# A spectral convolution on one core: the delayed odd spectrum by a table of phases on VectorE in place of a third second-step product

## The reference, cut to what matters

```python
def _stu_conv(phi, u, n):            # n = 8192
    sgn = +1 on even positions, -1 on odd ones
    Vf = rfft(phi, n); Uf_p = rfft(u, n); Uf_m = rfft(u * sgn, n)
    U_plus = irfft(Vf * Uf_p)[:sl];  U_minus = irfft(Vf * Uf_m)[:sl] * sgn
out = sum_k s_k (U_plus_k @ Mpp_k + U_minus_k @ Mpm_k) + sum_i shift(u, i) @ Mu_i
```

## Time and profile before

| what | us |
|---|---|
| median of 3 runs | 3136.38 |
| lowest and highest of them | 3129.91, 3153.72 |
| the profiled execution, its own time | 3149.02 |
| the span of its trace | 3147.3 |

### The profile page before, as it was taken

How to read it: one execution, slowest core, us unless ns; L and a number is a source line. 1 busy time by engine, 2 the same in 40 slices (tenths; PEclk the granted TensorE clock), 3 DMA queues, 4 the chain that set the end, 5 groups by cost and what they waited for, 6 DMA issues and landing times. The chain is left out here.

```text
span 3147.3 us, 88222 instructions
## 1 busy us (share of the span) xinstructions
PE 2528.9 (80%) x36744; PEld 1963.3 (62%) x36744; DVE 1538.8 (49%) x3563; ACT 1355.0 (43%) x2712; POOL 258.7 (8%) x477
## 2 busy tenths in 40 slices
PE   0565999545429999999999999999796884999999
PEld 0334888522128888888888888888633751555555
DVE  6441344233506565656565656565411343466666
ACT  0562344155016565656565656566410354232332
POOL 0102112000010000000000000000012001101000
PEclk9866899677859999999999999999998776799999
DMA  6437556422451111111111111110178520000000
GB/s 201 124 97 121 106 106 115 117 119 102 128 138 45 41 41 41 41 41 41 41 41 42 41 41 41 41 41 21 51 265 285 176 61 12 9 22 19 22 17 27
DMA packets 189043, 242.48 MB, mean 77 GB/s; under 512 B 36891, under 2 KB 147278, under 8 KB 185146
## 3 DMA queue, kind: packets, MB, share of 16 engines
q1 hardware_dynamic: 154325, 124.05, 14.7%
q0 software_dynamic: 30368, 94.52, 11.1%
q10 hardware_dynamic: 3969, 18.31, 1.5%
HBM read 145.54 MB, written 91.27 MB: 75 GB/s over the span
## 5 line engine op out<-in xcount | busy, mean ns | idle before, releaser
L962 DVE COPY spc_g<-spc_pz 128x512 f32<-128x512 f32 x1088 | 670.8, 683 | 446.8 <-PE spc_pz L860 446.7
L940 ACT ACTIVATE spc_g<-spc_pz 128x512 f32<-128x512 f32 x1088 | 587.2, 612 | 345.6 <-PE spc_pz L860 343.7
L860 PE MATMUL spc_pz<-spc_v,spc_as 108*128 108x128 bf16 x8704 | 599.9, 222 | 38.6 <-issue 27.7
L860 PEld LDWEIGHTS spc_pz<-spc_v,spc_as 108*128 108x128 bf16 x8704 | 515.2, 99 | 132.8 <-issue 46.0
L878 PE MATMUL spc_pz<-spc_g,spc_u 128*20 128x128 f32 x17408 | 503.7, 274 | 31.7 <-DVE spc_g L962 18.2
L878 PEld LDWEIGHTS spc_pz<-spc_g,spc_u 128*20 128x20 f32 x17408 | 480.0, 134 | 64.6 <-ACT spc_g L940 41.3
L1602 DVE SCALAR_TENSOR_TENSOR moe_yt<-moe_ex,moe_gb,moe_yt 128x128 f32<-128x128 f32 x768 | 209.6, 344 | 146.7 <-ACT moe_yt L1506 145.7
L845 PE MATMUL spc_pu<-spc_f,spc_s 128*128 128x256 f32 x816 | 222.6, 399 | 71.8 <-DMA spc_s<-s_sf 71.8
L1456 PE MATMUL moe_ex<-moe_ew,moe_d 128*128 128x512 f32 x512 | 254.0, 619 | 16.8 <-DVE moe_yt L1602 16.8
L507 DVE SCALAR_TENSOR_TENSOR inv_xo<-inv_pa,inv_mask,inv_xo 128x256 f32<-128x256 f32 x256 | 123.6, 484 | 222.7 <-PE inv_pa L465 163.9
L485 ACT ACTIVATE inv_b<-inv_pb 112x1024 f32<-112x1024 f32 x128 | 125.2, 1021 | 221.1 <-PE inv_pb L444 221.1
(11 more groups left out here) (195 smaller groups left out, 2407.6 us busy)
## 6 DMA issues: line engine op xcount, KB each, us to landing
s_yd<-spc_yo SPq DMA_DIRECT2D x136, 160.0 KB
spc_s<-s_sf POOLq DMA_DIRECT2D x36, 512.0 KB, 6.4
ivs_y<-s_yd POOLq DMA_DIRECT2D x34, 512.0 KB, 5.3
s_td<-ivs_to SPq DMA_DIRECT2D x34, 512.0 KB, 5.0
s_sf<-fwd_so ACTq DMA_DIRECT2D x16, 1024.0 KB, 5.4
ln_t<-s_td SPq DMA_DIRECT2D x32, 512.0 KB, 3.7
inv_x<-s_xn SPq DMA_DIRECT2D x88, 112.0 KB
inv_x<-s_xn POOLq DMA_DIRECT2D x88, 112.0 KB, 8.0
```

Source lines behind the costliest of these rows:

```text
L860: m = pe.matmul(pz[:, (p + 2) % 3, e // 4, 2 * FT * (e % 4):2 * FT * (e % 4) + 2 * FT], AS[:, x, 8 * p + e, :], V[:, k, x, :, FT * t:FT * ...
L940: act.activation(g_out(p, 0), g_in(p, 0), ACT.Copy).then_inc(ga, 1)
L962: v.tensor_copy(g_out(p, 1), g_in(p, 1)).then_inc(gd, 1)
```

## The change

The third spectrum is no longer a product. For each frequency and image the odd spectrum in slots 5 and 8 is multiplied by cos and sin of the frequency's angle (a new table `ph`, 128 x 2 x 128, loaded for every frequency), and the sums and differences give slots 3, 6 and 0: five DVE instructions, the helper `shifted`. Second steps per frequency go from 12 to 8, spread 3, 3, 2, 0 over the four units; the loads of `F` shrink from 4 KB to two pieces of 1 KB for each partition. `shifted` runs on DVE at the end of units 0 (image 0), 1 (image 1) and 2 (images 2 and 3), behind the unit's copies and, in unit 1, behind its four additions.

```diff
-    UB = 3 * NB
+    UB = 2 * NB
+    STEPS = ((0, 1, 2), (3, 4, 5), (6, 7), ())
+    AT = (4, 9, NPR - 1)
-        F = A.sb("f", [P, 2, 2, 4, NF2])
+        F = A.sb("f", [P, 2, 2, 2, NF2])
+        PH = A.sb("ph", [P, 2, NF2])
+        tmp = A.sb("tmp", [P, 2, 2, NF2])
...                                                      # POOL
+            def load_phases(f):
+                sp.dma_start(PH[:]..., one(I["ph"], f)).then_inc(in_p, 16)
...
+            load_phases(0)
             for k in range(2):
                 load_tokens(k, k)
                 load_filters(k, k)
...
                     sp.wait_ge(u_done, UB * (f + 1))
+                    sp.wait_ge(ph_ready, NB * (f + 1))
                     load_tokens((f + 2) % NF1, k)
+                    load_phases(f + 1)
                     sp.wait_ge(g_done, NPR * NUN * (f + 1))
                     load_filters((f + 2) % NF1, k)
...                                                      # PE, make_g
-                    if not last and p in (4, 9, NPR - 1):
-                        second_step(f + 1, 1 - k, 3 * (2 * t + x) + (4, 9, NPR - 1).index(p))
+                    for at, unit in zip(AT, STEPS[2 * t + x]):
+                        if not last and p == at:
+                            second_step(f + 1, 1 - k, unit)
...                                                      # PE, make_y
                 if t == 0 and x == 0:
                     pe.wait_ge(u_ready, UB * (f + 1) + 2)
+                    pe.wait_ge(ph_ready, NB * (f + 1))
...                                                      # ACT
-                            if not last and p in (4, 10):
-                                u_out(f + 1, 1 - k, 3 * (2 * t + x) + (4, 10).index(p))
-                        if not last:
-                            u_out(f + 1, 1 - k, 3 * (2 * t + x) + 2)
+                            for at, unit in zip(AT, STEPS[2 * t + x]):
+                                if not last and p == at:
+                                    u_out(f + 1, 1 - k, unit)
...                                                      # DVE
+            def shifted(f, k, b):
+                v.wait_ge(u_ready, 2 + UB * f + 2 * b + 2)
+                if b == 0:
+                    v.wait_ge(in_p, 16 * f + 16)
+                if not (isinstance(f, int) and f == 0 and b == 0):
+                    v.wait_ge(ph_ready, NB * f + b)
+                odd = U[:, k, 5:9:3, b]
+                for m in range(2):
+                    v.tensor_tensor(tmp[:, m], odd, PH[:, m:m + 1].to_broadcast([P, 2, NF2]), ALU.mult).then_inc(by_phase, 1)
+                v.wait_ge(by_phase, 2 * NB * f + 2 * b + 2)
+                v.tensor_tensor(U[:, k, 3, b], tmp[:, 0, 0], tmp[:, 1, 1], ALU.add)
+                v.tensor_tensor(U[:, k, 6, b], tmp[:, 0, 1], tmp[:, 1, 0], ALU.subtract)
+                v.tensor_tensor(U[:, k, 0, b], tmp[:, 1, 0], tmp[:, 0, 1], ALU.subtract).then_inc(ph_ready, 1)
+
+            for b in range(NB):
+                shifted(0, 0, b)
...                                                      # DVE, at the end of a unit
+                        if not last:
+                            for b in ((0,), (1,), (2, 3), ())[2 * t + x]:
+                                shifted(f + 1, 1 - k, b)
```

More of the change, by code:

```diff
@@ L239, in normalise_in @@
         reduced, red_ready = A.sem("reduced"), A.sem("red_ready")
-        passed = A.sem("passed")
         block = A.ctx.enter_context(nc.Block())
@@ L333, in _ @@
                     v.wait_ge(st_ready, D * i + k + 1)
-                    v.sem_inc(passed, 1)
                     for t in range(NT):
@@ L787, in spectrum @@
         u_done, u_ready = A.sem("u_done"), A.sem("u_ready")
+        in_p, by_phase, ph_ready = A.sem("in_p"), A.sem("by_phase"), A.sem("ph_ready")
         g_done, ga, gd = A.sem("g_done"), A.sem("ga"), A.sem("gd")
@@ L814, in load_filters @@
                                  one(S["VS"][part], f).rearrange("k x c f -> k (x c f)")).then_inc(in_v[k], 16)
+            def load_phases(f):
+                sp.dma_start(PH[:].rearrange("b s f -> b (s f)"), one(I["ph"], f)).then_inc(in_p, 16)
             def load_tokens(f, k):
-                sp.dma_start(F[:, k].rearrange("b p s f -> b (p s f)"), one(I["fw"], f)).then_inc(in_s[k], 16)
+                table = I["fw"].rearrange("n b (p m) -> n b p m", p=2)
+                sp.dma_start(F[:, k].rearrange("b p s f -> b p (s f)"), one(table, f)[:, :, 0:2 * NF2]).then_inc(in_s[k], 16)
                 for part in range(2):
@@ L835, in _ @@
                 sp.wait_ge(in_s[k], 48 * (NF1 // 2 + 1))
+            sp.wait_ge(in_p, 16 * NF1)
         @block.tensor
@@ L839, in second_step @@
             def second_step(f, k, unit):
-                b, g = divmod(unit, 3)
-                ph = 0 if g == 1 else 1
-                fo = 2 if g == 0 else 0
+                b, ph = divmod(unit, 2)
                 pe.wait_ge(u_ready, UB * f + unit + 1)
@@ L845, in second_step @@
                     m = pe.matmul(pu[:, unit % 2, 0:2 * NF2], Ss[:, k, part, b, ph * C:ph * C + C],
-                                  F[:, k, part, fo:fo + 2].rearrange("b s f -> b (s f)"),
+                                  F[:, k, part, 0:2].rearrange("b s f -> b (s f)"),
                                   start=part == 0, stop=part == 1)
@@ L923, in u_out @@
             def u_out(f, k, unit):
-                b, g = divmod(unit, 3)
+                b, g = unit // 2, unit % 2 + 1
                 act.wait_ge(u_done, UB * f + unit + 1)
@@ L1657, in tables @@
     fi = np.zeros((NF1, NF2, 3, P))
+    ph = np.zeros((NF1, P, 2, NF2))
     for f1 in range(NF1):
         f = f1 + 32 * f2
+        ph[f1] = np.stack([np.cos(2 * np.pi * f / 4096), np.sin(2 * np.pi * f / 4096)])
         for z in range(2):
@@ L1674, in tables @@
         "ident": np.eye(P), "cmat": np.eye(P) - 1.0 / C, "mask": np.kron(np.tile(np.eye(4), (2, 1)), np.ones((16, 1))), "d1": d1.reshape(P, 2 * P), "fw": fw.reshape(NF1, P, 8 * NF2),
-        "fi": fi.reshape(NF1, NF2, 3 * P), "d2": d2.reshape(P, 64),
+        "ph": ph.reshape(NF1, P, 2 * NF2), "fi": fi.reshape(NF1, NF2, 3 * P), "d2": d2.reshape(P, 64),
         "prio": np.tile(np.array([4.0, 3.0, 2.0, 1.0]), (P, 1)),
```

## The result

| | before | after |
|---|---|---|
| median of 19 runs each, us | 3146.31 | 3159.56 |
| ratio, with its 95% interval | | 1.0046 (1.0026 to 1.0066) |
| profiled execution: its time, span, us | 3149.02, 3147.3 | 3155.11, 3153.4 |
| `spectrum` stage in its trace, us | 1408.6 | 1409.6 |

The change makes the kernel slower by 0.46%, 14.5 us of 3146, by the ratio. With 19 runs the median of before is 3146.31, ten more than the three runs that the forecast started from; so ratios say more here than times. One run of before, of 3299.95 us, was in a slower state and does not count in the ratio. The stage is counted from the start of POOL's first load of it to the start of SP's last store.

The account below looks back on a forecast made before the run. DVE's 16 copies bound the first 11 us of a unit, PE's `make_y` the rest. Terms -14.4 + 20.5 - 2.8 = +3.3 us gave 3140 us on the median of 3136.38, no change; range 3125 to 3157.

Parts of the forecast that it names:

- unit 3, three steps fewer: Unit 3 of each looped frequency: without second steps 17.71 us instead of 18.61, 0.90 less, 16 times, -14.4 us.
- unit 2, the chain behind the additions: `shifted` behind unit 1's fourth addition delays unit 2's copies: 1.28 us per frequency, +20.5 us, bounds +16.2 and +30.6.
- ahead of the loop, rest: Before the first looped frequency: four of 12 second steps go and first tokens land earlier, -2.8 us, between 0 and -4.5.
- units 0 and 1: Both units stay at 18.6 us; unit 0's `shifted` costs nothing, lying in DVE's idle time behind its copies.
- D: Time by which one `shifted` on DVE holds back what follows: 1.43 us, between 1.31 and 1.91.
- The part that comes back: In unit 2, late DVE partly hides the first second step: bubble 0.25 instead of 0.45 us, 0.15 taken as returned.
- The turn of the loop: Rival, faster: 128 KB less transfer shortens the 7.9 us turn; -3 us by size, 3105 at most (large form, chance 0.03).
- the rival's estimate by size: At each loop turn, the token burst shortens by 0.4 us for 0.128 MB less, -3 us in 8 turns, 3137 us.
- The longer chain: Rival, slower: strided operands and waits lengthen DVE's `shifted`; from 3.2 us it costs +34 us, 3168 us, chance 0.04.
- The 25 us that the rule gave for the term: Unit 2's delay if each DVE instruction waits for an empty pipe: 1.72 us per `shifted`, 16 x 1.57; the forecast rejected it.

Follow-up runs that it names:

- loads_early: Changed kernel with POOL loading tokens and phase table at the end of unit 2, one unit ahead of the loop's turn: 0.9949 of before, stage 1399.4 us.
- image1_late: Changed kernel with image 1's chain moved from the end of unit 1 to unit 2, beside images 2 and 3: 0.9946 of before, stage 1391.9 us.
- image1_late_steps: Changed kernel with image 1's chain in unit 2 and unit 2's second steps behind groups 9 and 15, not 4 and 9: 0.9903 of before, stage 1385.6 us.
- image1_first: Changed kernel with image 1's chain still in unit 1, but ahead of the four additions instead of behind them: 0.992 of before, stage 1388.0 us.
- all_three: Changed kernel with image 1's chain in unit 2, its steps behind groups 9 and 15, and the early loads: 0.9849 of before, median 3104.20 us.

## Why the prediction was wrong

The forecast was 3140 us for a median of 3136, +3.3 us and no change; measured are a median of 3159.56, outside the range of 3125 to 3157, and a ratio of 1.0046. It was right on which unit pays and why, and wrong on the size of what unit 2 pays. Its term for unit 3 has the right size in part by luck.

| term | forecast | measured (means above) |
|---|---|---|
| unit 3, three steps fewer | -14.4 | -13.4 |
| unit 2, the chain behind the additions | +20.5 | +25.2 |
| ahead of the loop, rest | -2.8 | -3.9 |
| units 0 and 1 | 0 | +0.1 |
| stage | +3.3 | +7.9 |

**The step that failed** is the price in unit 2, "1.43 - 0.15 = 1.28 per frequency". D was right: 1.40 measured. Two things were wrong about what follows it.
- *The part that comes back* does not: behind the first second step DVE idles 0.37 us as before, so 1.41 are paid (12.94 against 11.53), 2 us more in 16. My count chained group 4 to the end of copy 1; in the trace groups 3 and 4 follow each other without a wait (16 products in 1.21 us), and the same 0.37 is left.
- *The granted clock* was missing, a cost put at nothing without a reason. I had PE stop at group 3 and took it to go on at full speed. 21 of 80 times it did not, at 1.5 us each, 4.2 x 1.5 = 6.3 us per execution; three more falls behind the wait ahead of `make_y`, at 1.8 us each, are 1.1 us. The earlier trace rows showed the clock at 0.5 behind a wait of 4.33 us, and I used them only for the turn of the loop. I had no row of a wait of 1.5 us within the groups, and did not bound what the clock might cost there.

These make 2.1 + 6.3 + 1.1 = +9.5. Against it, `make_y` in unit 2 of before is interrupted, in part to wait for issue, for some 5.6 us in all (304.8 - 16 x 18.70), and in after for 0.7 (330.0 - 16 x 20.12 - 7.4). 20.5 + 9.5 - 4.9 = 25.1, which is the measured term.

**Unit 3**: 17.65 us where nothing disturbs it, as forecast, and its `make_g` is 0.90 us shorter everywhere (10.48 for 11.38). But the total of -13.4 is not made of 16 times that. The means of one unit 3, by frequency:

| us | before (3 traces) | after (5 traces) | in all |
|---|---|---|---|
| the 8 even frequencies | 18.57 | 18.61 | +0.3 |
| the 7 odd ones, each ahead of a turn | 24.68 | 22.92 | -12.3 |
| the last one of the loop | 19.05 | 17.65 | -1.4 |

In the even frequencies nothing is earned: `make_y` takes 8.12 us there instead of 7.19, and gives the 0.9 back. At the turns the unit earns twice the forecast. That the three rows add up to nearly -14.4 is luck. The interruptions of `make_y` that unit 2 lost turn up in unit 3. That they moved because the place of `make_y` in PE's code moved is argued, not shown.

**Ahead of the loop**: near the forecast, and by the reasons given: the groups come 4.7 us earlier in the first pair of traces, the copies 3.1. The late copies show as PE's wait of 1.52 us in unit 0 of frequency 0, which takes 20.1 us where it took 18.55; these 1.5 us stand in the row of units 0 and 1.

**The rivals.** The turn of the loop did move, which the prediction had named as a sign of being wrong. From unit 1 to the next unit 1, a frequency with a turn takes 82.24 us where it took 82.73, and one without 76.74 where it took 75.05 (means of five and three traces); so a turn costs 5.5 us and not 7.7, more because the others got longer than because it got shorter. Ahead of a turn `make_y` with the wait behind it takes 12.5 us where it took 13.3, 0.8 less, and 0.4 was the rival's estimate by size. Whether the smaller table does this is not shown. loads_early shows that the transfers matter: 16 us, for 1.5 MB moved away from the turn.

The longer chain: behind the additions D is 1.40. The 128x256 product takes 0.42 us beside the groups (34 of them in the trace of after) and 0.53 on average beside `make_y` (87 of them), which explains the mean of 493 ns; beside `make_y` it is hidden. No wait of DVE in the stage is put down to issue. The Trainium skill ("VectorE: DVE Perf Modes", section "The DRAIN you can't avoid"), taken as a rule for every instruction, would have had D at 1.72; the trace has 1.40, with the sums 0.21 apart at 0.29 each, so the rows decide against that use of it. The same section adds that a next instruction that is not held starts earlier, and with this the rows agree. The 25 us that the rule gave for the term is what unit 2 measured, by coincidence: D was not 1.72.

The Trainium skill ("TensorE: Matmul & The Clock Gate", section "What's actually happening") says that the array's clock is throttled by default and that activity releases it. The traces agree with the second half: the granted clock of before is 1.00 from 2211.24 to 2228.95, a unit without steps with its wait of 1.19 us, and it falls behind some waits of 1.47 us and nearly all of 3 us. The three falls behind a wait of 1.18 us came in units that already had one of 1.47 us.

**What stays open.** The stage explains 7.9 us; the whole kernel was measured at +14.5, between 8.2 and 20.8. The rest may be scatter: the involution stage took 353 to 373 us in the five traces of after, 342 to 375 in three of before. In the five timed kernels that keep the change's other parts, the whole lies below before by 0 to 8 us more than the stage does (image1_late -17.0 and -16.7, image1_late_steps -30.5 and -23.0, image1_first -25.2 and -20.6, loads_early -16.0 and -9.2, all_three -47.5 and -45.3), which speaks against a loss outside it. What decides behind which of the equal waits the clock falls is open. A further 10 us of the missed median belong to the three runs of before that it started from.

## What to carry to other kernels

Work moved to an engine with 40% to spare is free only in that engine's idle stretch; ask for every piece which instruction stands right behind it, and who waits for that one. The same five instructions cost 29 us behind the last addition and nothing ahead of the first. Price a new wait of TensorE not only by its length: look for rows that show what its clock did after waits of that length, and where there are none, put the lower level into the range.

## What the runs showed of the hardware

- Behind equal waits of PE of 1.47 us the granted clock fell to the 1.2 GHz level in 21 of 80 cases and stayed up in 59 (6 of 16 in loads_early); behind waits of 3.0 us it fell in 14 of 16. A fall costs 1.5 us and more: the four fp32 matmuls 128 x 256 of a second step take 2.02 us instead of 1.08. Three times in the 80 it fell behind the wait of 1.18 us that follows 9 us later.
- PE's wait at a turn of this hardware loop scatters beside the 1.5 MB of transfers: 2.8 to 7.2 us in the three traces with the stage as before, 4.5 to 6.3 in the five of after. With the transfers moved away (loads_early, all_three) it is 2.9 to 3.5 us in all 14 turns.
- VectorE's instructions take longer beside `make_y`, the small fp32 products of PE, than beside the bf16 products: 0.53 against 0.42 us for a 128x256 product of two SBUF operands, 0.89 against 0.69 for an addition 128x512 with an operand in PSUM (trace of after).
- One stage of unchanged code took 342 to 375 us in 14 traces, with mean granted clocks of 0.77 to 0.85 in its stretch in the eight read for it; unit 1 of `spectrum` repeated within 0.6 us in 16 frequencies, and the stretch of the last stage from its first `moe_ex` product to the last store of the output took 451 to 452 us in all 14.
